# A graph layer and an expert layer on one core: a unit's first products join the second products of the unit ahead, and 7 groups are computed ahead instead of 6

## The reference, cut to what matters

```python
# x: 12500 x 256, 200000 edges (src, dst, edge_weight) sorted by dst; float32 throughout
support = layernorm(x) @ W
x = x + segment_sum(support[src] * edge_weight[:, None], dst) + b
# expert layer over xn = layernorm(x): 8 experts, 256 -> 512 -> 256
logits = mean(xn, over all rows) @ Wr + br      # one decision for all 12500 rows
# softmax, a cap on the load, softmax, the 2 best experts and their weights w
h = gelu(xn @ W1[e] + b1[e]);  y[e] = h @ W2[e] + b2[e]
x = x + layernorm(sum over the 2 experts of w[e] * y[e] + xn) * gamma + beta
```

## Time and profile before

| | |
|---|---|
| median of three runs | 2519.41 us |
| the profiled execution, its own time | 2519.76 us |
| its span in the trace | 2518.0 us |
| gather stretch: last gather issued, last edge matmuls end | 1989.6 us, 1996.4 us |
| post stretch: first `down` matmul | 2041.5 us |
| TensorE busy, weight loads busy | 2178.6 us, 1651.2 us |
| GpSimd busy | 1656.8 us |
| ScalarE busy, VectorE busy | 1145.3 us, 1054.8 us |
| granted clock of TensorE, mean | 0.96 |

### The profile page before, as it was taken

How to read it: one execution, slowest core, us unless ns; L and a number is a source line. 1 busy time by engine, 2 the same in 40 slices (tenths; PEclk the granted TensorE clock), 3 DMA queues, 4 the chain that set the end, 5 groups by cost and what they waited for, 6 DMA issues and landing times. The chain is left out here.

```text
span 2518.0 us, 40482 instructions
## 1 busy us (share of the span) xinstructions
PE 2178.6 (87%) x9536; PEld 1651.2 (66%) x9537; DVE 1054.8 (42%) x2962; ACT 1145.3 (45%) x3139; POOL 1656.8 (66%) x1643
## 2 busy tenths in 40 slices
PE   2388898889989988899989989889899889888898
PEld 1266666666767665676666666666676678777787
DVE  7693222232332232232232223223233257778876
ACT  3467666565564444443333233322311265544453
POOL 6577777777777777777777777777777413434332
PEclk9899999999999998999999999999999989999999
DMA  9955555555655555555555546555555422322221
GB/s 339 305 163 163 164 166 162 170 176 173 222 183 177 162 173 158 172 174 172 161 164 168 165 149 193 161 161 166 171 165 172 131 97 93 101 84 84 84 77 54
DMA packets 229382, 401.22 MB, mean 159 GB/s; under 512 B 35813, under 2 KB 150170, under 8 KB 229244
## 3 DMA queue, kind: packets, MB, share of 16 engines
q0 software_dynamic: 75072, 205.10, 27.5%
q1 hardware_dynamic: 153740, 192.37, 23.7%
q10 hardware_dynamic: 432, 2.40, 0.3%
HBM read 323.27 MB, written 76.46 MB: 159 GB/s over the span
## 5 line engine op out<-in xcount | busy, mean ns | idle before, releaser
L515 POOL DMA_INDIRECT G<-xr_d,SRC x1468 | 1390.9, 947 | 447.2 <-issue 297.3
L970 DVE TENSOR_SCALAR OH<-CST,DL,WR 128x128 f32<-128x128 f32 x1564 | 571.0, 371 | 1273.5 <-PE ps L1240 747.0
L1240 PE MATMUL ps<-G,OH 128*128 x3128 | 744.7, 390 | 141.6 <-DVE OH L970 130.1
L1240 PEld LDWEIGHTS ps<-G,OH 128*128 128x128 f32 x3128 | 597.3, 194 | 283.6 <-issue 204.6
L1219 PE MATMUL ps<-YU,W1u 128*128 128x512 f32 x768 | 358.6, 620 | 58.6 <-ACT H L697 31.1
L1230 PE MATMUL ps<-W2u,H 128*128 128x256 f32 x1536 | 347.4, 385 | 7.2 <-issue 6.9
L1230 PEld LDWEIGHTS ps<-W2u,H 128*128 128x128 f32 x1536 | 292.4, 192 | 58.6 <-issue 19.5
L1219 PEld LDWEIGHTS ps<-YU,W1u 128*128 128x128 f32 x768 | 147.7, 198 | 248.5 <-issue 207.3
L704 ACT ACTIVATE YE<-ps 128x512 f32<-128x512 f32 x96 | 57.3, 597 | 445.9 <-PE ps L1230 445.9
L697 ACT ACTIVATE H<-ps,b1a 128x512 f32<-128x512 f32 x192 | 130.9, 687 | 275.6 <-PE ps L1219 275.4
L1072 DVE TENSOR_TENSOR Hlo<-Ht,Hhi 128x512 fp32r<-128x512 f32 (+1 forms) x152 | 135.5, 898 | 115.7 <-ACT Hhi L796 115.6
(11 more groups left out here) (170 smaller groups left out, 2494.5 us busy)
## 6 DMA issues: line engine op xcount, KB each, us to landing
W1u<-in_W SPq DMA_DIRECT2D x48, 512.0 KB
W2u<-in_W SPq DMA_DIRECT2D x48, 512.0 KB
y_d<-YE SPq DMA_DIRECT2D x48, 512.0 KB
G<-xr_d,SRC POOLq DMA_INDIRECT x1468
x_d<-X SPq DMA_DIRECT2D x98, 128.0 KB, 2.5
yt_d<-YT SPq DMA_DIRECT2D x98, 128.0 KB, 2.4
XR<-in_x SPq DMA_DIRECT2D x97, 128.0 KB
XS<-in_x SPq DMA_DIRECT2D x24, 512.0 KB, 12.9
```

The costliest lines, as they stand in the source:

```text
L515: e.indirect_dma_start(out=G[:, s % RING, :], out_offset=None, in_=x if s < FRESH else xr_d, in_offset=bass.IndirectOffsetOnAxis(ap=SRC[:, ...
L970: e.tensor_scalar(OH[:, s % OHR, :], iota, DL[:, s:s + 1], WR[:, s + 1:s + 2], ALU.is_equal, ALU.mult).then_inc(s_oh, 1)
L1240: e.matmul(ps[:, 0, 0:D], OH[:, r, :], Gf[:, bass.ds(g + r * D, D)], start=False, stop=True, skip_group_check=True).then_inc(s_main, 1)
```

## The change

A unit's first products and the second products of the unit ahead of it form one event, BOTH: DOWNS of unit n - 1, then UPS of unit n. The first event of the series is a UPS alone and the last a DOWNS alone. AHEAD goes from 6 to 7, so units from 48 to 56, and post groups from 19 to 18. Before there were 96 unit events, now there are 57. They are spread over tiles by the same rule. In tile 96 there were 3 units (6 events), now 4 BOTH; in tile 97 there were 7 units (14 events), now 7 BOTH and the DOWNS. The GELU output H now lies in its buffer from one event to the next. SyncE loads W2u of unit n when the DOWNS in the event BOTH of n is through, and W1u of unit n + 1 when its UPS is.

```diff
--- before.py
+++ after.py
@@ -19,13 +19,13 @@
 
 GT = 4
 NG = (NT + GT - 1) // GT
-AHEAD = 6
+AHEAD = 7
 UNITS = AHEAD * E
 HID = 2 * F // P
 HB = 4
 VIRTUAL = 4
 FINAL = NT - 1 + VIRTUAL
-END, EXTRA, UPS, DOWNS = range(4)
+END, EXTRA, UPS, BOTH, DOWNS = range(5)
 
 
 def tiles(g):
@@ -56,10 +56,11 @@
     room = [max(0.0, 0.75 * slots[t] - 3.5) if t >= 18 else 0.0 for t in range(NT)]
     free, u, out = 0.0, 0, []
     for t in range(NT):
-        free += room[t] * UNITS / sum(room)
-        n = max(0, min(int(free + 0.5), UNITS - u)) if t < NT - 1 else UNITS - u
+        free += room[t] * (UNITS + 1) / sum(room)
+        n = max(0, min(int(free + 0.5), UNITS + 1 - u)) if t < NT - 1 else UNITS + 1 - u
         free -= n
-        mine = [(round(64 * (k + 1) / (2 * n + 1)) / 64, kind, u + k // 2) for k, kind in enumerate([UPS, DOWNS] * n)]
+        kinds = [UPS if k == 0 else DOWNS if k == UNITS else BOTH for k in range(u, u + n)]
+        mine = [(round(64 * (k + 1) / (n + 1)) / 64, kind, u + k) for k, kind in enumerate(kinds)]
         if t == NT - 1:
             mine += [(k / 32, EXTRA, NT - 1 + k) for k in range(VIRTUAL)]
         out += [(t, *m) for m in sorted(mine)]
@@ -401,18 +402,18 @@
                 store_x(l)
             e.dma_start(b1a[:, :, :], b1t.rearrange("e p f -> p e f")).then_inc(b1_in, 16)
             for t, _, kind, n in EVENTS:
-                if kind == UPS:
+                if kind in (BOTH, DOWNS):
+                    if n < UNITS:
+                        load_w2(n)
+                    keep_y(n - 1)
+                if kind in (UPS, BOTH):
                     if n + 1 < UNITS:
                         load_w1(n + 1)
                     if n % E == E - 1 and n + 1 < UNITS:
                         load_yt((n + 1) // E)
                     if n == E:
                         e.dma_start(W1A[:, :, :, :], W1.rearrange("e (c p) n -> p e c n", p=P)).then_inc(w1a_in, 16)
-                elif kind == DOWNS:
-                    if n + 1 < UNITS:
-                        load_w2(n + 1)
-                    keep_y(n)
-                else:
+                if kind in (END, EXTRA):
                     keep_rows(n)
                     if n == GT + 2:
                         for l, lot in enumerate(lots):
@@ -729,11 +730,11 @@
                 seed_x(l)
                 scale_x(l)
             for t, _, kind, n in EVENTS:
-                if kind == UPS:
+                if kind in (BOTH, DOWNS):
+                    unit_out(n - 1)
+                if kind in (UPS, BOTH):
                     unit(n)
-                elif kind == DOWNS:
-                    unit_out(n)
-                else:
+                if kind in (END, EXTRA):
                     section(n)
 
             def high(k):
@@ -1252,11 +1253,11 @@
                             begin(v, g + (r - 1) * D)
                         e.reg_add(v_r, v_r, 1)
                     with e.Else():
-                        with e.If(now == UPS):
-                            unit_up(e.snap(u_r, min_val=0, max_val=UNITS - 1))
-                        with e.Else():
+                        with e.If(now > UPS):
                             unit_down(e.snap(u_r, min_val=0, max_val=UNITS - 1))
                             e.reg_add(u_r, u_r, 1)
+                        with e.If(now < DOWNS):
+                            unit_up(e.snap(u_r, min_val=0, max_val=UNITS - 1))
                     e.reg_mov(rel, e.snap(due) - a)
 
             def slots(a, g, n):
```

## The result

The changed kernel takes 2510.48 us in the median of seven runs (2508.27 to 2514.59), the kernel before, run beside it and earlier, 2521.9 us (seven runs). The ratio is 0.9954, with a 95% interval of 0.9943 to 0.9966: 11.4 us less. I had forecast no change, 2521 us. By its time it is my first rival, TensorE keeps up (2509 us), to which I had given 0.24, and not the forecast. The profiled execution is one of 2508.27 us with a span of 2506.5, against 2519.76 and 2518.0 before.

A forecast was written before the change was run, and what follows sets the result against it. GpSimd's gathers were taken to bound the gather stretch, TensorE close behind. Last edge 13 us later, post stretch 12.7 us shorter, plus an odd microsecond of ScalarE waits, on 2519.76 us gave 2521 us; range 2507 to 2534 us.

The forecast's parts named there:

- first rival: End of gather stretch: TensorE keeps up, last edge 0 to 5 us later, post stretch gives 12.7 us, 2509 us; chance 0.24.
- What bounds it: Gather stretch: GpSimd's gathers at 1.252 us each set its length; TensorE, 90.5% busy, keeps up with little to spare.
- One event for two: Unit events: merging removes the 31.1 us GELU wait, 15 us of half clock and 14 us of issue and event gaps.
- Sum: 60 us saved: TensorE in the gather stretch: total saving from merging events, of GELU waits, half clock and gaps.
- Net load: 112 - 60 = +52: Gather stretch: eight more units less the merge's saving, in us, against a cushion of 60.2 us; it just fits.
- Where it does not fit: From tile 96's first BOTH: 274.0 us of TensorE work against 262.9 us of gathers, so the last edge comes 13 us later.
- the state with the work piled up: Last tiles: reason for taking 13 us, as the rows giving the 0.38 us event gap show this state.
- my lower bound of 4 us: Last edge's lateness at least: zero gap, sections of 2 us, nothing left over from tile 95; upper bound 27 us.
- SyncE's transfers: W2u and W1u loads: over 10 us between request and need, a load moved within 3.3 us, so costed at nothing.
- The post stretch: After the gathers: one post group less, -22.6 us, one group read back more, +9.9 us, together -12.7 us.
- The sum: Whole kernel: +13 - 12.7 = +0.3 us on 2519.76, with an odd microsecond of ScalarE waits put on it, 2521 us.
- points (2) and (6): Checks: last gather to end of last edges 20 us, not 6.9; post stretch 12.7 us shorter; wrong if sum is off over 8.

The follow-up runs named there:

- experiment 4: Changed kernel with 8 groups ahead and not 7, events still merged: 2575.17 us, ratio 1.0218 to the kernel before.
- experiment 3: Changed kernel with UPS of unit n ahead of DOWNS of the same unit in one event, 7 groups: 2566.97 us, ratio 1.0179 to the kernel before.
- experiment 1: Changed kernel with 6 groups ahead as before, so the merge into BOTH alone: 2519.21 us, ratio 0.9986 to the kernel before.
- experiment 2: Kernel before with 7 groups ahead and not 6, UPS and DOWNS still separate events: 2543.32 us, ratio 1.0086.
- experiment 5: Changed kernel with room of tiles 96 and 97 scaled by 0.9 or 0.8, moving events earlier: 2509.78 and 2509.34 us; changed kernel again 2511.77.

## Why the prediction was wrong, point by point

**What bounds it** was right: GpSimd's pace held within 0.7 us, and TensorE has little to spare; the lag of 67.8 us in experiment 4 shows it.

**One event for two** was right in mechanism: the GELU wait and the gap ahead of UPS are gone, and experiment 3 shows that the wait goes because of the order. It was wrong as a sum. Of "Sum: 60 us saved" the waits came as I had them: 30.7 us for the GELU (I took 31.1) and 14.1 of issue gaps (I took 14). The term that failed is the 15 us of half clock: UPS gave 20.8, but edges and DOWNS took some 26 back at their old counts, and sections waited 8.7 more, so experiment 1 gives 29 us. "Net load: 112 - 60 = +52" erred the other way by more: eight units took 62 us of cushion and lag, not 112, as there is less waiting and less half clock with them. The cushion went down by 28 us and not by 52. In both I held the granted clock at what the rows showed while I changed the waits ahead of the work.

**Where it does not fit** is the step that failed for the forecast. It gave +13 us, and +3.9 were measured. The work from the first BOTH of tile 96 was to take 274.0 us; from 1729.49 to 2000.15 it took 270.7. Most of these 3.3 us are the gaps, which are zero ahead of most events: the timeline has one of 0.25 and one of 0.47 us, and I had 0.38 for each of twelve. The larger part is the starting lag, the term that I mis-sized most: I took TensorE to be 6.9 + 2 us behind its gathers at the start of tile 96, 6.9 being the lag at the end of the kernel before. It had just waited 2.92 us for a one-hot matrix there, and 1729.49 is 3.5 us behind 1988.91 - 262.9 = 1726.0, 4 us with the odd pauses of the gathers: 5 us less than I took. The last gather was 0.7 us earlier as well. I had called it "the state with the work piled up", and the trace has it piled up only from tile 96 on.

That my lower bound of 4 us is what came is luck. The bounds were added up wrongly: with the values named for them the lower is (90.7 + 160.8 + 10) / 0.99 - 262.9 = 1 us, the upper 32 us and not 27. And the lower one keeps the start 6.9 us behind, on which it hung: the work ran 270.7 - 262.9 = 7.8 us over its gathers, not 4, but from a start 3.5 us behind.

**SyncE's transfers** at nothing: right, no wait for W1u or W2u stands among TensorE's waits in the changed kernel.

**The post stretch** gave 16.2 us and not 12.7. Up to the fifteenth post group it took what it did before; the seventh group read back falls among the last four post groups, and cost 21.9 - 16.5 = 5.4 us, not 9.9 (21.9 us is a post group near the end of the kernel before, from 2461.50 to 2483.39 in its chain). I had priced it as one in the middle; there was no row for one at the end. The price at the end holds: from the fifteenth post group to the end the traces with 7 groups of experiments 2, 3 and 5 take 84.5 to 86.0 us, this one 85.9. The part ahead of it doesn't: 374.5 to 380.6 us. So the whole gave 10 to 17 us, and 16.2 is near its upper end.

**The sum**: +4.7 - 16.2 = -11.5 in place of +0.3. The lateness accounts for 8.3 us of the miss, counted at the first `down`, the post stretch for 3.5. By my own sign I was wrong: points (2) and (6) together are off by 12 us, more than 8. The first rival gave 2509 us by "0 to 5 us later", and 3.9 us lies in it. Its mechanism came only in part: TensorE did not have its work done within the gathers, it ran 7.8 us over them, and part of its number is the longer saving of the post stretch. My argument against it, that the excess is 4 us even at zero gap, was no argument: 4 us later is inside the rival.

## What to carry to other kernels

When work is put behind a fixed-rate producer, don't subtract matmul time from the sum of waits. In this kernel the half clock came and went with the waits for the producer: work that filled them cost less than its matmuls, and work saved gave back less. Ask for every such stretch where TensorE stands at its start, and not only how much work is in it. Take a marginal price from two kernels that differ only in the amount (here 7.8 us for a unit of 14.0, then 11.1). Order independent work ahead of a product that waits for another engine; putting two events into one is worth little by itself. And a kernel filled to the last microsecond of such a cushion was faster only where the same engine was the bound: run it on more than one chip before it is kept.

## What the runs showed that I had not expected

- One chip ran the kernel before in 3130.6 us and others in 2522 to 2524 us. The gathers took the same 0.946 us; ScalarE and VectorE stood for releases for which the trace has no cause, VectorE for 437.2 us ahead of the one-hot matrices, and TensorE and GpSimd behind them.
- Saved waiting was in part given back as half clock: the merge alone took 45 us of GELU wait and issue gap away, and the mean granted clock fell from 0.97 to 0.96, although TensorE idled 11 us less in all. With 7 groups it was 0.98 in all three forms, also where no wait for one-hot matrices was left but one for the GELU was (experiment 2), and with 8 it was 0.99.
- Taking away a 55.3 us wait for one load on ScalarE moved 50.2 us of it onto another load, and the stretch got no shorter.
